# Products that nobody reads on TensorE, in the list part and ahead of the experts' first turn

## What is computed

```python
t = x * rsqrt(mean(x * x) + EPS) * norm_scale          # 4096 rows of 256
logits = t @ gate_w + gate_b                           # 8 experts
top_v, top_i = top_k(logits, 2)
w = zeros((T, 8)).at[arange(T)[:, None], top_i].set(softmax(top_v))
for each expert e:                                      # (256 -> 1024, swiglu -> 512 -> 256)
    h = swiglu(t @ mlp1_w[e] + mlp1_b[e])
    acc = acc + w[:, e, None] * (h @ mlp2_w[e] + mlp2_b[e])
```

## Time and profile before

| | |
|---|---|
| median of 3 runs | 1742.53 us |
| lowest and highest | 1741.09, 1742.98 us |
| the profiled execution's own time | 1741.74 us |
| its span | 1740.0 us |
| TensorE busy, share of the span | 1625.0 us, 93% |
| VectorE busy | 1268.9 us, 73% |
| ScalarE busy | 1046.8 us, 60% |
| GpSimd busy | 797.8 us, 46% |
| granted TensorE clock, mean | 0.955 of full speed |

### The profile page before, as it was taken

The page is one execution under the profiler, slowest core; times in us unless marked ns, Lnnn a source line. Parts: engine busy times, 40 slices in busy tenths (PEclk is TensorE's granted clock), DMA queues, the critical chain, the costliest instruction groups (busy, mean ns, idle before and its releaser), DMA issues. The chain is left out here.

```text
span 1740.0 us, 35905 instructions
## 1 busy us (share of the span) xinstructions
PE 1625.0 (93%) x11174; PEld 1195.6 (69%) x11175; DVE 1268.9 (73%) x2639; ACT 1046.8 (60%) x1847; POOL 797.8 (46%) x780
## 2 busy tenths in 40 slices
PE   8989999999999886999999998899965999999998
PEld 4544444444442675999999997445445999999997
DVE  5788888888882676777777775478876777777775
ACT  4437777677777454666666664557664666666663
POOL 4541111112112132666666664325642666666664
PEclk9999999999999886999999999899965999999999
DMA  5754445354431871322222333301121222332222
GB/s 164 193 148 115 114 112 129 93 138 111 118 94 50 170 243 46 69 48 46 48 46 48 49 48 48 94 1 49 49 84 58 43 49 48 48 48 49 47 46 36
DMA packets 102683, 140.85 MB, mean 81 GB/s; under 512 B 18176, under 2 KB 86784, under 8 KB 99520
## 3 DMA queue, kind: packets, MB, share of 16 engines
q1 hardware_dynamic: 65282, 90.53, 20.0%
q0 software_dynamic: 31808, 37.32, 13.4%
q10 hardware_dynamic: 5502, 11.88, 1.9%
HBM read 74.21 MB, written 56.69 MB: 75 GB/s over the span
## 5 line engine op out<-in xcount | busy, mean ns | idle before, releaser
L596 ACT ACTIVATE a_Pt<-a_p_st 128x512 f32<-128x512 f32 (+2 forms) x624 | 302.4, 593 | 128.8 <-PE a_p_st L676 128.2
L622 DVE TENSOR_REDUCE mx<-a_p_sn 128x2 f32<-128x256 f32 (+1 forms) x600 | 333.4, 628 | 60.3 <-PE a_p_sn L659 50.8
L1383 ACT COPY R<-values_then_w 128x1024 f32 x284 | 283.0, 1044 | 41.8 <-issue 21.4
L1332 PE MATMUL e_p_g<-e_tT,R 128*128 128x128 f32 x2272 | 280.6, 277 | 1.6 <-issue 0.9
L1332 PE MATMUL e_p_l<-e_tT,R 128*128 128x128 f32 x2272 | 276.9, 275 | 0.0
L1344 PE MATMUL e_p_y<-w,e_hid 128*128 x1136 | 269.5, 380 | 5.8 <-DVE e_hid L1452 5.8
L1332 PEld LDWEIGHTS e_p_g<-e_tT,R 128*128 128x128 f32 x2272 | 268.3, 194 | 2.5 <-issue 1.3
L1332 PEld LDWEIGHTS e_p_l<-e_tT,R 128*128 128x128 f32 x2272 | 265.4, 192 | 0.1
L573 POOL TENSOR_SCALAR_AFFINE_SELECT a_Pt<-a_Pt 128x512 f32<-128x512 f32 x128 | 81.2, 635 | 360.4 <-ACT a_Pt L596 360.4
L1344 PEld LDWEIGHTS e_p_y<-w,e_hid 128*128 128x128 f32 x1136 | 205.2, 191 | 28.2 <-issue 6.2
L659 PE MATMUL a_p_sn<-Kst,Qst 96*128 96x128 bf16 (+1 forms) x720 | 219.2, 331 | 2.2 <-PEq L161 1.8
(11 more groups left out here) (226 smaller groups left out, 2364.2 us busy)
## 6 DMA issues: line engine op xcount, KB each, us to landing
qk_parts<-a_part SPq DMA_DIRECT2D x64, 192.0 KB, 3.2
a_Vst<-values_then_w SPq DMA_DIRECT2D x16, 512.0 KB, 18.5
values_then_w<-in_mlp SPq DMA_DIRECT2D x16, 512.0 KB, 4.6
t_rows<-R SPq DMA_DIRECT2D x16, 512.0 KB, 3.2
Kst<-qk_parts SPq DMA_DIRECT2D x14, 384.0 KB
Qst<-qk_parts SPq DMA_DIRECT2D x14, 384.0 KB
o_rows<-a_OT ACTq DMA_DIRECT2D x16, 256.0 KB, 2.0
o_rows<-xs ACTq DMA_DIRECT2D x16, 256.0 KB, 8.2
```

The costliest lines, as they stand in the source:

```text
L596: act.activation(weights(kb, slice(h, h + n), a, b), p_st[:, i % RING, 0:n * (b - a)].rearrange("p (n w) -> p n w", n=n), ACT.Exp, scale=D ...
L622: dve.tensor_reduce(mx[:, hs[0]:hs[-1] + 1, place], p_sn[:, (s + k) % RING, 0:w * len(hs)].rearrange("p (h w) -> p h w", w=w), AX.X, ALU.m ...
L1332: mm = pe.matmul(bank[:, s, c * P:(c + 1) * P], copied[:, s, k, at:at + P], tT[:, s, k * P:(k + 1) * P], start=(k == 0), stop=(k == KD - 1))
L1383: act.copy(copied[:, s, :, cols], g["w1"][:, bass.ds(e, 1), :, cols].rearrange("p a k n -> p (a k) n")).then_inc(copied_done, 1)
```

## The change

A helper `unread` issues products of `identb` with itself, four times side by side, 128 x 128 weights and 512 columns in bf16. In the list part they go to a bank of PSUM of their own (`p_unread`), in the expert stage to `p_y[:, 1, :]`, which turn 1 writes later. They have no semaphore: nobody waits for them, and they wait for nobody. There are 13 as the first thing in the list part, 14 behind the eight small products for `expert` and ahead of the inversion, 4 behind the products of each of the five groups, and 8 at the start of the expert stage.

```diff
+def unread(pe, g, bank, count):
+
+    for _ in range(count):
+        pe.matmul(bank, g["identb"][:, :], g["identb"][:, :].unsqueeze(1).to_broadcast([P, 4, P]),
+                  start=True, stop=True, skip_group_check=True)
...
+    p_unread = mem.ps("p_unread", [P, 512])
...
         @block.tensor
         def _(pe):
+            unread(pe, g, p_unread[:, :], 13)
             pe.wait_ge(picks_done, 1)
...
             mm.then_inc(expert_done, 1)
+            unread(pe, g, p_unread[:, :], 14)
             for k in range(GROUPS):
                 pe.wait_ge(mark_done, k + 1)
                 pe.wait_ge(row_done, k + 1)
...
                 mm.then_inc(inv_done, 1)
+                unread(pe, g, p_unread[:, :], 4)
...
+            unread(pe, g, p_y[:, 1, :], 8)
             rows(0, 0, True)
```

## The result

The changed kernel takes 1750.52 us (median of 6 runs, 1748.62 to 1753.17), where the kernel before took 1742.76 us in the 6 runs beside it (1741.09 to 1744.64). The ratio is 1.0043, with a 95% interval of 1.0033 to 1.0053: slower by 0.4%, where I had forecast 0.3% faster. The profiled execution took 1752.55 us, with a span of 1750.8.

A forecast was written before the change was run, and what follows sets the result against it. It took half clock around the list parts and first turns as the bound, with the list part mostly VectorE's. Gains of 2 x 0.9 + 2.0 + 1.9 = 5.7 us gave 1736.8 us, range 1734.2 to 1741.0.

The forecast's parts named there:

- my 4.0: Start of the list part and first turn: unread products raise the clock some 4.0 us after the first one starts.
- They cost nothing, as I had said: List part ahead of the inversion: the 13 and the 14 hold nobody up, price 0.
- I take 0.058 us for a list product instead of 0.123.: Inversion at full clock: list products speed up to 0.058 us each, bringing the token list 0.9 us earlier.
- My upper bound, 0.123: Inversion: upper bound for a list product at full clock, in us, meaning nothing gained.
- rival B: Inversion: weight loads stay at 0.123 us whatever the clock; token list 0.7 us late, 1740.0 us in all; chance 0.07.
- C, slower: Inversion: clock falls between groups, long products go at half clock; 2 us lost a stage, 1746.5 us; chance 0.08.
- its point of decision: Inversion: the slower case decides if the clock is at half in two groups or more.
- Rival A: Expert stage start: clock is down again, first products 0.5 us later, 1.6 us won a stage, 1739.4 us; chance 0.17.
- The first turn: Experts' first turn at full clock: 3.79 us instead of 5.82, gain 2.0 us; second stage gain 1.9 us.
- It just fits, with no slack left: First turn: turn 2's gather, taken as 3.05 us, lands at 684.2, against transposes that want it at 684.27.
- the product at its lower bound of 0.030 us: Inversion: list product with the weight load hidden, said to bring 0.2 us more a stage.

The follow-up runs named there:

- probe: Rows of 16 short products, moving operand dense or stepped, added at the list part's start without the rest of the change; full clock: 0.033 us dense, 0.131 at 32 bytes.
- `bias_early`: The whole change, with the eight second-layer bias loads moved from the expert stage's start to the list part's start; 1751.56 us, ratio to before 1.0046.
- `eight_only`: The kernel before plus only the eight unread products ahead of the experts' first turn; 1744.46 us, ratio to before 1.0006.
- `fours_only`: The kernel before plus only the four unread products behind each group, without 13, 14 and 8; 1754.52 us, ratio to before 1.0063.

## Why the prediction was wrong

- **What was missed, in us.** I forecast 5.7 us won and measured 7.8 lost. Of these 13.5 us the list parts make 7.8 (1.8 won in the forecast, 6.0 lost in the profiles) and the first turns, up to turn 4, make 5.8 (3.9 won in the forecast, 1.9 lost).
- **The clock.** The 13 raised it in the first list part (at 656.5, 2.9 us after their start, sooner than my 4.0); in the second all 13 ran at half clock, and it rose at 1318.7, 5.4 us after their start. It fell as the 14 began or shortly after (663.3, 1322.1), and during the 14 it rose again (666.7, 1325.5). They cost nothing, as I had said. That it would then stay up was right in the first list part and wrong in the second.
- **The list product at full clock: this step failed.** "I take 0.058 us for a list product instead of 0.123." It was 0.13 at full clock. I took the value from a pair of 128-column products, because they too have a weight load each. That was the wrong likeness: their moving operand is dense, and that of the list product has a step of 32 bytes (probe: 0.033 against 0.131 us at full clock). My upper bound, 0.123, was near the truth.
- **What the bound would have cost: rival B was mis-sized.** It said 0.7 us late for each list part. It only looked at groups 3 and 4. A group of 16 at 0.123 with its four takes 2.84 us by its own numbers, above VectorE's 2.44 for group 2 and 2.17 for group 3. The delay adds up from group 1 on: 2.2 us at full clock, 3.8 where the clock falls. By its mechanism B is what happened in the first list part; I had given it a chance of 0.07.
- **C, slower, was the outcome by sign.** Its mechanism (a clock that falls in the inversion) accounts for the 1.6 us by which the second list part is later than the first. The first list part is 2.2 us late with the clock up throughout, so its point of decision, half clock in two groups, was met in the second list part only and was not needed for a loss. Rival A did not occur in the changed kernel: both its expert stages began at full clock.
- **The first turn.** That its products would follow the clock was right (1.89 us from `e_p_g` to the next transposes instead of 3.58). "It just fits, with no slack left" was wrong: I took 3.05 us for turn 2's gather from turn 0's, which was the first to be issued, 1.4 us ahead of the first bias load. Turn 2's took 4.8 and 5.4 us (685.59 to 690.40, 1346.81 to 1352.21). Turn 2 came 0.37 us earlier and 0.55 us later after the token list, instead of 2.0 and 1.9 us earlier. After the wait of 2.05 us the clock fell in the second stage, which made turn 2 there 1.7 us longer. That the bias loads lengthen the gather is supported by `bias_early` (4.1 and 4.0 us), but not settled: it is still a microsecond over my 3.05, and a pause without a named releaser stands there too.
- **The Trainium skill's rule on the weight load.** The Trainium skill (TensorE: Matmul & The Clock Gate, "LDWEIGHTS (loading the stationary operand)") would have 0.107 us for each product at either clock, and the inversion without a gain, which is how it came out. The probe shows that this was for another reason: with 128 weights and a dense operand the products are 0.033 us apart at full clock.
- **Slips in the working that don't bear on the outcome.** By its own terms the product at its lower bound of 0.030 us would bring 0.7 us a stage (16 x 0.028 + 8 x 0.028), not 0.2, and rival A's first products would start at 681.7, not 681.85.

What stays open: what lengthens turn 2's gather, why four engines stand together in turn 2 when the first turn is quick, and how much of the gain of the first turn could be had without that.

## What to carry to other kernels

Before you buy clock for a stretch, check that its products follow it. The sure sign is a row of the same shape, step included, at both clocks; the number of columns and the weight load are not enough. Products that nobody reads are free only in time that the engine surely has left over. Ahead of a wait that is long at either clock (13 and 14 here) they cost nothing; the 8 end within 0.3 us of the coming of turn 0's rows at full clock, and 1.7 us late at half (`eight_only`). Between groups that VectorE delivers every 2.2 to 2.4 us, and which take 2.07 themselves, what the fours take beyond the rest adds up over the groups. And the time of the first gather of a stage (3.05 us) is no price for a later one (4.8 and 5.4 us here), which has other gathers and 1 MB of loads beside it.

## What was not expected of the hardware

- The moving operand's step sets the time of a list product, apart from the clock: 71 columns of bf16 take 0.033 us dense, 0.066 with a step of 8 bytes and 0.131 with 32 bytes at full clock; 0.057, 0.067 and 0.130 at half. A step of 4 bytes costs next to nothing (0.059 and 0.034).
- VectorE's bf16 operations kept their speed when the broadcast operand was repeated over the middle dimension and the innermost one was a pair (0.73 us for 1136 elements, as before).
- The same four products behind each group raised or held the clock in one kernel and not in another: half clock through groups 1 to 4 in `fours_only`, full clock through all groups in the first list part of the change, a fall between groups 1 and 2 in its second.
